# Whole-block probability transposes in attention, and other engines issuing the loads of the routed experts' stage

## What is computed

```python
# attention, 16 heads of 128
entries = einsum('bcr,bcrh->bch', softmax(x @ Wcmp), x by 4 tokens)   # 512 compressed entries
ck, cv = rope(rmsnorm(entries @ Wk)), entries @ Wv
sc = where(block_ends <= pos, q @ ck.T * scale, NEG)
tv, ti = top_k(sc, 8); pw = softmax over the 8, others 0
ctx_sparse = pw @ cv
ctx_local = softmax(q @ k.T over this and the previous 128 tokens) @ v
x = layernorm(x + ((ctx_sparse + ctx_local) * 0.5) @ Wo)
# feed-forward: 16 routed experts (4 picked of each token), 2 shared ones, 352 hidden
x = layernorm(x + sum over picked e of w_e * (silu(x @ w1[e]) * (x @ w3[e])) @ w2[e] + shared(x))
```

## Time and profile before

| | |
|---|---|
| median of three runs | 2321.15 us (2320.03 to 2322.51) |
| the profiled execution, its own time | 2319.89 us |
| its span, first to last instruction | 2318.1 us |
| attention's 256 steps | about 70 to 1460 us of the span |
| router and early shared experts | about 1460 to 1664 us |
| routed experts | 1664 to 2200 us |
| combine | 2200 to 2318 us |
| TensorE, VectorE, ScalarE, GpSimd busy | 2186.9, 1453.3, 1195.9, 1441.2 us |
| mean granted TensorE clock | 0.975 |

### The profile page before, as it was taken

One profiled execution on the slowest core, in us unless ns is written; L12 is line 12 of the kernel. 1 busy time (PEld: TensorE's weight loads), 2 busy tenths in 40 slices (PEclk: granted clock), 3 DMA queues, 4 the chain that ended last, 5 costly groups with the idle time before them and its releaser, 6 DMA issues. The chain is left out here.

```text
span 2318.1 us, 43243 instructions
## 1 busy us (share of the span) xinstructions
PE 2186.9 (94%) x13185; PEld 1973.6 (85%) x13186; DVE 1453.3 (63%) x4382; ACT 1195.9 (52%) x3946; POOL 1441.2 (62%) x2027
## 2 busy tenths in 40 slices
PE   6899999999999999999999999899999999979873
PEld 4799999999999999999999998477799999968852
DVE  5678778778778778778778778473222222212266
ACT  2566666666666666666666667521133333322221
POOL 2787667667667666666666666466562203799576
PEclk9999999999999999999999999999999999989976
DMA  5600530000000000000000000334353323566366
GB/s 147 205 22 19 184 112 20 3 22 22 1 22 22 2 22 22 3 20 22 9 14 22 1 1 2 100 112 165 117 171 111 110 91 115 174 185 183 121 182 181
DMA packets 87881, 177.23 MB, mean 76 GB/s; under 512 B 11600, under 2 KB 40976, under 8 KB 87568
## 3 DMA queue, kind: packets, MB, share of 16 engines
q1 hardware_dynamic: 55808, 84.93, 11.8%
q0 software_dynamic: 19504, 69.23, 9.8%
q10 hardware_dynamic: 12384, 20.80, 2.4%
HBM read 107.80 MB, written 67.13 MB: 75 GB/s over the span
## 5 line engine op out<-in xcount | busy, mean ns | idle before, releaser
L961 PE MATMUL bank<-whi,xT_lo 128*128 128x384 f32 x1024 | 366.7, 358 | 4.3 <-PEq L180 3.2
L814 POOL TENSOR_TENSOR cross<-nat,rope_tables 128x128 f32<-128x128 f32 x256 | 111.9, 437 | 407.6 <-DVE nat L663 407.6
L963 PE MATMUL bank<-whi,xT_hi 128*128 128x384 f32 x1024 | 345.2, 337 | 0.0
L962 PE MATMUL bank<-wlo,xT_hi 128*128 128x384 f32 x1024 | 345.1, 337 | 0.0
L740 ACT COPY probT<-bank 128x128 f32<-128x128 f32 (+3 forms) x256 | 109.5, 428 | 330.4 <-PE bank L576 330.2
L961 PE MATMUL bank<-ring_hi,xslo 128*128 128x352 f32 x600 | 202.8, 338 | 18.3 <-issue 16.9
L1632 DVE TENSOR_TENSOR shlo<-bank,shhi 128x256 fp32r<-128x256 f32 x76 | 32.3, 425 | 296.4 <-ACT shhi L1600 296.4
L676 DVE SCALAR_TENSOR_TENSOR prob<-taken,prob 128x32 f32<-128x32 f32 (+15 forms) x256 | 217.4, 849 | 0.9 <-ACT prob L751 0.8
L663 DVE TENSOR_TENSOR nat<-bank,bqk 128x256 f32<-128x256 f32 x256 | 108.8, 425 | 169.0 <-PE bank L963 168.7
L607 PE MATMUL bank<-probT,cv 128*128 128x128 f32 (+3 forms) x1280 | 206.5, 284 | 3.6 <-ACT probT L742 3.6
L961 PEld LDWEIGHTS bank<-whi,xT_lo 128*128 128x128 f32 x1024 | 193.5, 189 | 5.0 <-issue 3.4
(11 more groups left out here) (270 smaller groups left out, 6431.8 us busy)
## 6 DMA issues: line engine op xcount, KB each, us to landing
staged<-in_wexp POOLq DMA_DIRECT2D x64, 544.0 KB, 4.3
slots_in<-zeros SPq DMA_DIRECT2D x41, 512.0 KB, 6.6
xslot<-slots_in SPq DMA_DIRECT2D x76, 256.0 KB, 2.7
slots_out<-yslot ACTq DMA_DIRECT2D x76, 256.0 KB, 2.0
wraw<-in_wh SPq DMA_DIRECT2D x16, 768.0 KB, 4.3
staged<-in_wexp SPq DMA_DIRECT2D x16, 544.0 KB, 3.8
slots_out<-zeros SPq DMA_DIRECT2D x9, 512.0 KB, 6.2
acc<-in_x SPq DMA_DIRECT2D x4, 1024.0 KB, 12.0
```

The costliest lines, as they stand in the source:

```text
L814: pool.tensor_tensor(cross[:, :, :], nat[:, a.two, :, 0:2 * ROT], sin, ALU.mult).then_inc(s_mult, 1)
L961: pe.matmul(out, wl_, xh_, start=first, stop=False)
L962: pe.matmul(out, wh_, xl_, start=False, stop=False)
L963: return pe.matmul(out, wh_, xh_, start=False, stop=last)
```

## The change

The last block of the selected probabilities is transposed and multiplied whole. VectorE writes zeros into the columns of `prob` from `width` to the end of the block ahead of L645, in the tiles whose last block isn't full. In the routed stage SyncE issues the weight quarters' loads, under the wait that GpSimd had for them, and ScalarE issues the x tiles' loads, each behind its copy of the high half of the x tile before; there is one x load more, which nothing on TensorE reads. The bound of the register value of `first_tile` goes down by one.

```diff
-    def entries(tile, b):
-
-        return min(P, width(tile) - b * P)
...
         for b in range(blocks(a.tile)):
-            rows = entries(a.tile, b)
-            pe.transpose(b_turn_s[0:rows, b * P:(b + 1) * P], pr[:, b * P:b * P + rows], ident[:, :])
+            pe.transpose(b_turn_s[:, b * P:(b + 1) * P], pr[:, b * P:(b + 1) * P], ident[:, :])
...
-        parts = [(cv[0:entries(a.tile, b), b, :], probT[0:entries(a.tile, b), b * P:(b + 1) * P])
-                 for b in range(blocks(a.tile))]
+        parts = [(cv[:, b, :], probT[:, b * P:(b + 1) * P]) for b in range(blocks(a.tile))]
...
         wait_for(dve, s_turn, n - KEEP + 1)
+        if w < blocks(tile) * P:
+            dve.memset(prob[:, a.slot, w:blocks(tile) * P], 0.0)
         dve.tensor_tensor_reduce(pl[:, lc], local(a), mask, 1.0, NEG, ALU.add, ALU.max,
...
             @block.sync
             def _(sp):
-                def load(g):
-                    r = sp.snap(g * P)
-                    sp.wait_ge(s_xt, g - 1)
-                    sp.dma_start(x[:, :], xs[bass.ds(r, P), :]).then_inc(x_in, 16)
-
-                with sp.Fori(1, first_of(sp, E)) as g:
-                    load(g + 1)
+                for f in range(2, LAST + 1):
+                    for q in range(QUARTERS):
+                        sp.wait_ge(s_w, (f - 1) * QUARTERS + q + 1)
+                        sp.dma_start(staged[:, quarter(q)], t["wexp"][f, :, quarter(q)]).then_inc(st_in[q], 16)
...
-                        if f < LAST:
-                            pool.wait_ge(s_w, QUARTERS + done)
-                            pool.dma_start(staged[:, quarter(q)], t["wexp"][f + 1, :, quarter(q)]).then_inc(st_in[q], 16)
...
-                pool.wait_ge(x_in, end * 16)
+                pool.wait_ge(x_in, end * 16 + 16)
...
+                def load(g):
+
+                    r = act.snap(g * P)
+                    act.dma_start(x[:, :], xs[bass.ds(r, P), :]).then_inc(x_in, 16)
+
...
                 x_high(1)
+                load(2)
                 end = first_of(act, E)
                 with act.Fori(1, end) as g:
                     act.wait_ge(s_u1, g)
                     act.activation(gate[:, :], b_u1[:, 0:INTER], ACT.Silu).then_inc(s_silu, 1)
                     h_high(g)
                     x_high(g + 1)
+                    load(g + 2)
                     y_store(g)
```

More of the change, by code:

```diff
@@ L1484, in first_of @@
         def first_of(eng, e):
-            return eng.value_load(first_tile[0:1, e:e + 1], min_val=e + 1, max_val=MAXT - 1)
+            return eng.value_load(first_tile[0:1, e:e + 1], min_val=e + 1, max_val=MAXT - 2)
         def staged_in(eng, f, q):
```

## The result

The median is 2265.7 us against 2320.6, a ratio of 0.9763 (95% interval 0.9746 to 0.978): 54.9 us less, where 43.6 were forecast. The profiled execution took 2264.9 us, its span is 2263.1.

What follows compares the result with a forecast made beforehand. Bound by TensorE's matmuls in attention and GpSimd's weight preparation in the routed stage; 35.8 - 0.3 + 8.1 = 43.6 us off the profiled 2319.9 gives 2276.3, as a median 2277.5 us; range 2271 to 2288.

Steps and rivals of the forecast that it cites:

- The bound: TensorE's own row of matmuls in attention; among the routed experts, GpSimd, behind TensorE's waits of 8.00 and 8.90 us.
- The sum's first term: Attention: contexts of 32 or 64 rows cost 0.28 us more; 128 steps at full rows take 35.8 us off TensorE.
- rival 3: Attention: row count has no price, the 0.28 us comes from the block's place in the order; 2313.3 us, chance 0.03.
- Nothing hides it: Attention: the whole 35.8 us arrives, because TensorE has no idle time there.
- Zeros: Attention: 192 zero writes on VectorE, mostly covered, cost 0.3 us in all, 6.4 us at most.
- The cover: Attention's tightest step: low halves end 0.32 us ahead of the scores, 0.15 where TensorE waited, leaving 0.17 us.
- Rival 1: Attention: zeros and shorter steps use up VectorE's 0.17 us of cover, scores come late; 2283.6 us, chance 0.10.
- Weights: Routed stage: without the loads GpSimd's quarters shorten from 4.60 to 3.72 to 3.77 us; the stage ends 8.1 us earlier.
- the ring place of expert 11: Routed stage: free only when expert 7's last tile is through; this lets expert 11 start 2.3 us earlier.
- Rival 2: Routed half does nothing: ring place or landing of the weights sets experts 11 and 12; 2285.6 us, chance 0.05.
- The loads of x: Routed stage: issued by ScalarE where it sits idle 1.59 us, instead of by SyncE; costed at zero.
- Rival 4: Routed stage: an x tile issued by ScalarE lands late, beyond 5.9 us; with 1 us more 2352.5 us, chance 0.04.

Runs made afterwards that it cites:

- e5: The changed kernel with at least 96 rows in the last block instead of 32 or 64, and 128 zero writes instead of 192: 2263.4 us, ratio 0.9749.
- e10: The changed kernel with 64 rows in the last block where it had 32, its own number otherwise, and 64 zero writes: 2308.3 us, ratio 0.9945.
- e14: The changed kernel without the zero writes of each step, prob cleared once at the start: 2262.4 us, ratio 0.9752.
- e9: The changed kernel with each zero write followed by one as wide into a tile that nothing reads: 2268.5 us, ratio 0.9777.
- e3: The kernel before with only the x tiles' loads moved from SyncE to ScalarE, the weights' loads still on GpSimd: 2320.6 us, ratio 1.0001.

## Why the prediction was wrong

**The bound** was read rightly: TensorE's row of matmuls in attention (in heads 1 to 14), and GpSimd behind two waits of the routed stage.

**The sum's first term is what failed.** "Costs 0.10 + 0.18 = 0.28 us more" is 0.38: the working compared the distances up to the first matmul of v and took the rest of the row as equal, while v's first two matmuls stand 0.10 us further apart behind a short block. 128 x 0.38 is 49 us in place of 35.8. That the price is there at 32 and 64 rows and gone at 96 was right, e5 and e10 show it, and rival 3 falls.

But not all of the 49 us arrived. "Nothing hides it, because TensorE has no idle time there" fails at three places. First, in heads 1 to 14 a head got 41.1 / 14 = 2.94 us where 8 x 0.38 is 3.08 (unrounded); 0.11 of the missing 0.14 is the late scores of tile 3. Second, in head 0 TensorE stands waiting anyway (4.4 us for the low halves before the change, 5.2 after), and what lies ahead of head 1 got 1.4 us of its 3.1. Third, at the end it waits as well, most of all for ScalarE's copies of the probabilities (3.6 us before, 4.0 after): the last context comes 93.2 to 93.3 us behind the scores of head 15 in both kernels, and the stretch up to the routed stage is 1.2 us longer. That 1.2 is within what this stretch varies by, 298.3 to 300.9 us; why it varies, no run shows. So 41.3 us is the outcome of two misses, a price 0.10 us too small in 128 steps (13 us) and 8 us that did not arrive, and that the term came as near as 5.8 us is partly luck.

**Zeros.** Priced at 0.3 us, worth 0 in e14. The cover was estimated at 0.17 us at the tightest step of the kernel before; that it does not reach for two sets is e9. Rival 1 named the right place, the scores behind the low halves, but of its two causes only the shorter steps count, for 0.11 us a head or 1.6 us in 14 heads, not 6.1. The tightest step of the kernel before was the wrong one to look at: the step of tile 3 had 0.50 us, more than the 0.32 of the earlier trace rows, and 0.38 of it was taken away, because it is one of the steps that got shorter.

**Weights.** The mechanism was right, and the size nearly: a quarter 3.65 us for 3.72 to 3.77, the ring place of expert 11 the new limit, TensorE's waits 3.06 and 6.01 us for 3.5 and 6. GpSimd at expert 11, and TensorE's two waits, in the changed kernel:

```profile
2008.32 0.19 POOL L1510 TENSOR_TENSOR spare<-spare 128x1 f32<-128x1 f32 x1 [9.23 <-PE bank L959]
2008.44 1.09 POOL L1514 CAST ring_hi<-staged 128x1088 fp32r<-128x1088 f32 x1
...
2012.08 1.11 POOL L1514 CAST ring_hi<-staged 128x1088 fp32r<-128x1088 f32 x1
```

```profile
2024.67 0.43 PE L957 MATMUL bank<-ring_hi,xslo 128*128 128x352 f32 x1 [3.06 <-issue]
...
2039.21 0.66 PE L957 MATMUL bank<-ring_hi,xslo 128*128 128x352 f32 x1 [6.01 <-issue]
```

GpSimd now stands 9.23 us in front of expert 11 until TensorE is through with expert 7, where it stood 0.24 before. Expert 11 starts 2051.97 - 2008.32 = 43.65 us earlier, 2.35 more than the stage itself, for the 2.3 predicted; seven quarters at 0.95 us less instead of 0.83 make the rest, and TensorE's second wait ends 8.9 us earlier. (Two slips of the prediction here are small: by the earlier trace rows the idle time began at 2070.98 - 8.00 = 2062.98, not 2062.8, and 2.3 + 3 x 0.83 is 4.8, not 4.7.) The mean clock of the window from 2000 to 2100 us rose from 0.90 to 0.95 with the shorter waits. Rival 2 falls.

**The loads of x** were priced at zero, and e3 measures zero. Rival 4 falls.

**The term that the sum did not have** is GpSimd's closing DRAIN, 5.287 - 0.040 = 5.25 us. The idle time of 28.72 us in front of the first gather, "issue" by name, was in the trace before; the prediction looked at what the loads cost beside the weights' arithmetic and not at what GpSimd leaves behind for the end of the block.

In numbers: 43.6 forecast, 5.8 more up to the routed stage, 0.6 more in it, 5.3 for the DRAIN, 0.3 less after it, is the 55.0 us between the two spans. With either the DRAIN or the surplus of attention alone the time would have been 2271.0 to 2271.5 us, at the edge of the range; it took both to leave it.

## What to carry to other kernels

When a matmul's shape has a price, measure it from the last undisturbed matmul in front to the second one behind: the row that showed the missing third was one line further than the earlier trace rows. Where an engine's DMAs are moved away, look also at the end of the block, at the sequencer's rows and at idle time ended by "issue". Where TensorE's own row gets shorter, each of the shortened steps takes as much from the cover of the chain beside it: compare the cover of those very steps, here 0.50 - 0.15 = 0.35 us at tile 3 against 0.38, and not that of the tightest step of the kernel before. And an engine's share says little: VectorE, at 81 of 100 without the zeros (943.22 us of 1160 in e14), took 192 writes of 0.11 us in the mean for nothing, and not another 192.

## What was not expected of the hardware

- A pair of float32 matmuls with 32 or 64 contraction rows, among others with 128, makes four weight loads come late, its own two and the two behind it, for 0.38 us in all at the full clock; 96 rows cost what 128 do.
- GpSimd's DRAIN at the end of the routed block lasts 0.040 us plus 0.082 us for each load it issued in the block: 0.137, 1.367 and 5.287 us for 1, 16 and 64, wherever in the block they were issued. The router's block, with 64 scattering stores by GpSimd, has one of 5.286 us as well, before and after the change, but it ends at 1653.1 us there and VectorE's at 1664.2, so it costs nothing.
- The formula holds where GpSimd has nothing else under way. Attention's block, without a DMA by GpSimd, ends with a DRAIN of 0.657 us; it started together with an instruction of 0.55 us. The last block, with 64 gathers, has 5.881 us before the change, again with an instruction of 0.55 us, and it ends 0.2 us before the span does; the next engine, SyncE, was done 2.1 us ahead of it. What another issuer of the gathers would bring was not run.
